# A conditioned four-layer sequence kernel: the first layer's query and key weights loaded as eight transfers instead of two

## The reference, cut to what matters

```python
mod = silu(c) @ W_mod + b_mod                    # six vectors of 128 per batch
sh_msa, sc_msa, g_msa, sh_mlp, sc_mlp, g_mlp = split(mod, 6)
h = layernorm(x) * (1 + sc_msa) + sh_msa
q, k, v = split(h @ W_qkv, 3)                    # 16 heads of 64
x = x + g_msa * (softmax(q k^T / 8) v @ W_out + b_out)
x = x + g_mlp * ff(layernorm(x) * (1 + sc_mlp) + sh_mlp)
```

## Time and profile before

| | |
|---|---|
| three runs, device time | 498.73, 500.25, 500.51 us; median 500.25 |
| the profiled execution, device time | 498.17 us |
| its span, first to last instruction | 496.4 us |
| mean granted TensorE clock in it | 0.965 of full speed |
| busy: PE, PEld, DVE, ACT, POOL | 410.4, 261.3, 310.9, 280.1, 175.7 us |
| moved by DMA | 21.25 MB |

### The profile page before, as it was taken

How to read it: one execution, slowest core, us unless ns; L and a number is a source line. 1 busy time by engine, 2 the same in 40 slices (tenths; PEclk the granted TensorE clock), 3 DMA queues, 4 the chain that set the end, 5 groups by cost and what they waited for, 6 DMA issues and landing times. The chain is left out here.

```text
span 496.4 us, 9353 instructions
## 1 busy us (share of the span) xinstructions
PE 410.4 (83%) x3196; PEld 261.3 (53%) x3196; DVE 310.9 (63%) x846; ACT 280.1 (56%) x596; POOL 175.7 (35%) x226
## 2 busy tenths in 40 slices
PE   4767788898889998889988788787688889799965
PEld 4534454555546555455545455445355666666644
DVE  4656776764573455726475766867688877675621
ACT  2333344375453846346755776456568566877754
POOL 7503211331263331774379222723133322321210
PEclk9999899999999999999997989879899999999997
DMA  6860033000000000120013030001222313210000
GB/s 160 303 61 2 9 30 48 1 1 1 0 1 2 1 1 12 45 73 2 0 33 85 13 101 27 3 1 41 87 75 87 96 34 98 82 59 12 3 12 11
DMA packets 34527, 21.25 MB, mean 43 GB/s; under 512 B 22832, under 2 KB 31408, under 8 KB 34096
## 3 DMA queue, kind: packets, MB, share of 16 engines
q1 hardware_dynamic: 34480, 20.65, 16.1%
HBM read 16.97 MB, written 3.67 MB: 42 GB/s over the span
## 5 line engine op out<-in xcount | busy, mean ns | idle before, releaser
L917 ACT ACTIVATE pt<-psum 128x512 f32<-128x512 f32 (+1 forms) x192 | 106.2, 558 | 95.5 <-PE psum L1514 47.2
L1121 DVE TENSOR_REDUCE negm<-psum 128x2 f32<-128x512 f32 x128 | 84.6, 683 | 38.5 <-PE psum L1443 24.7
L703 POOL TENSOR_TENSOR pairsum<-pt 128x256 f32<-128x256 f32 x64 | 46.8, 732 | 143.6 <-ACT pt L917 140.2
L714 POOL COPY big<-mT 32x1024 bf16<-32x1024 bf16 x32 | 33.2, 1038 | 119.4 <-ACT mT L909 119.0
L1489 PE MATMUL psum<-big 128*128 128x256 bf16 (+1 forms) x256 | 50.8, 268 | 4.8 <-POOL big L714 3.7
L1118 DVE TENSOR_REDUCE negm<-psum 128x3 f32<-128x384 f32 x64 | 34.8, 554 | 15.1 <-PE psum L1449 14.4
L1509 PE MATMUL psum<-big 64*128 64x256 f32 x256 | 40.1, 404 | 2.5 <-ACT pt L917 2.4
L1162 DVE TENSOR_TENSOR oT<-psum,rden 128x256 f32<-128x256 f32 x64 | 26.5, 415 | 18.8 <-ACT rden L933 18.2
L1538 PE MATMUL psum<-pt,room 128*64 128x256 f32 x256 | 35.6, 400 | 0.0
L1412 PE MATMUL psum<-hT,pt 128*128 128x256 f32 x128 | 33.3, 396 | 1.4 <-DVE negm L1121 1.3
L1538 PE MATMUL psum<-pt,vpad 128*32 128x256 f32 (+1 forms) x512 | 32.5, 373 | 1.6 <-DVE oT L1162 1.6
(11 more groups left out here) (184 smaller groups left out, 858.9 us busy)
## 6 DMA issues: line engine op xcount, KB each, us to landing
big<-scratch SPq DMA_DIRECT2D x96, 96.0 KB
scratch<-room SPq DMA_DIRECT2D x48, 64.0 KB, 2.0
adj_s<-adj SPq DMA_DIRECT2D x16, 110.0 KB, 3.7
w0s<-w SPq DMA_DIRECT2D x1, 1536.0 KB, 8.3
w3s<-w SPq DMA_DIRECT2D x1, 1088.0 KB, 10.9
room<-wqk SPq DMA_DIRECT2D x2, 512.0 KB, 6.3
xT<-x_t SPq DMA_DIRECT2D x4, 128.0 KB, 2.2
w1s<-w SPq DMA_DIRECT2D x1, 512.0 KB, 8.9
```

Source lines behind the costliest of these rows:

```text
L703: nc.gpsimd.tensor_tensor(pairsum[:, u % SUM_RING, :], pt[:, pt_slot(u), 0:T], pt[:, pt_slot(u), T:2 * T], ALU.add).then_inc(pairsum_ready, 1)
L714: nc.gpsimd.tensor_copy(stacks[SHIFT_ROW:128, b % ROOMS, 0, GH * g:GH * (g + 1), :], mT[SHIFT_ROW:128, at % 2, :].unsqueeze(1).broadcast_t ...
L917: nc.scalar.activation(pt[:, pt_slot(u), 0:width], psum[:, ST_BANK + u % 2, 0:width], ACT.Exp, scale=EXP_SCALE[layer]).then_inc(pt_ready, 1)
L1121: ins = nc.vector.tensor_reduce(negm[:, g, 0:NT, j], bk.rearrange("p (q k) -> p q k", q=NT), AX_X, ALU.max, negate=True)
```

## The change

The two transfers become eight. Each carries four heads of the queries or of the keys: 64 rows of 2 KB, 128 KB in all. They are issued in the order queries 0 to 3, keys 0 to 3, queries 4 to 7, and so on. The one semaphore becomes four, one for each group of four heads, and `turn_weights(n)` waits for its own group's two transfers alone. SP still waits for all eight before it goes on.

```diff
-        wqk_in = sem("wqk_in")
+        wqk_in = [sem(f"wqk_in{n}") for n in range(W_PARTS)]
...
-                for s in range(2):
-                    sp.dma_start(wqk0s[s * DH0:(s + 1) * DH0], wqk0[:, s]).then_inc(wqk_in, 16)
-
-                sp.wait_ge(wqk_in, 16 * 2)
+                for n in range(W_PARTS):
+                    heads = slice(H // W_PARTS * n, H // W_PARTS * (n + 1))
+                    for s in range(2):
+                        sp.dma_start(wqk0s[s * DH0:(s + 1) * DH0, heads], wqk0[:, s, heads]).then_inc(wqk_in[n], 16)
+
+                for n in range(W_PARTS):
+                    sp.wait_ge(wqk_in[n], 16 * 2)
...
                 def turn_weights(n):
 
-                    pe.wait_ge(wqk_in, 16 * 2)
+                    pe.wait_ge(wqk_in[n], 16 * 2)
                     wait_s_bank_free(pe, "W", n)
```

## The result

| | before | after |
|---|---|---|
| median of 22 runs each, us | 499.13 | 497.24 |
| ratio, 95% interval | | 0.9946 (0.9923 to 0.997) |
| profiled execution, us (span) | 498.17 (496.4) | 494.97 (493.2) |
| mean granted clock in it | 0.965 | 0.969 |

The ratio leaves out the slow runs of either kernel (four of the 22 of after) and says 0.54% less time, 2.7 us (1.5 to 3.8); over all 22 of each the medians differ by 1.9 us. Forecast were 1.3 us, 0.26%. The direction and the place were right, the forecast size was half of what the ratio says.

What follows compares the result with a forecast made beforehand. The head was taken to be bound by PE's 1.92 us wait for the query and key weights, then DVE. A shift of 1.3 us, taken between 1.1 and 1.4, gave 500.25 - 1.3 = 498.9 us, range 496.8 to 500.8.

Steps and rivals of the forecast that it cites:

- Where the gain comes from: PE behind first_mods: its 1.92 us standstill is its only wait on the query and key weights.
- Landings (part 1): Query and key transfers: eight issues take 3.8 us; pairs land no later than 6.9, 8.2, 9.5 and 10.8.
- Rival (a): Small transfers do not overlap, so turn_weights(3) waits; last lands at 19, kernel 6 us later at 506.3 us; chance 4%.
- The most that this edit can give is 1.92 us: Upper bound at the head of the chain: PE's whole idle time from 8.05 to 9.97.
- Part 2: PE's turning of the weights: transposes from 8.05, third group 10.2 to 11.3, ACT's second copy from 12.98 to 11.4.
- part 3: DVE is late next: vectors until 10.39, xn until 11.03, unmoved; last weight loads at 11.8, first product at 12.7; shift 1.3 us.
- DVE in the way whatever lands: Argument against a larger gain: DVE is occupied from 8.10 to 11.03 however early the weights land.
- rival (c): Faster by over 0.5%: the whole 1.92 us arrives and low-clock stretches fall better, about 497 us; chance 14%.
- The clock: Granted at 1.00 (2.4 GHz) in the first 30 us; low-clock stretches can differ by execution and cause spread.
- part 4: Everything behind the first product follows: no later wait is ended by SP's transfers or POOL, so the shift reaches the end.
- The sum: Whole kernel: no PE, DVE or ACT instruction added or removed; 500.25 - 1.3 = 498.9 us, a gain of 0.26%.
- What a measurement can tell: Measurement of this kernel: about 0.5% (2.5 us) can be told from no change; the runs' spread is 1.8 us.

Runs made afterwards that it cites:

- e1: Changed kernel with its eight transfers, but the first group of transposes waits for all four pairs; ratio to before 0.9988 (0.9949 to 1.0026).
- e5: Changed kernel once more, unedited, for a second profile; ratio to before 0.9984 (0.9942 to 1.0025).
- e6: Changed kernel with eleven more identity transposes in PE's earlier idle times; ratio to before 0.995 (0.9924 to 0.9975).
- e8: Changed kernel with eleven more identity transposes on PE and six small DVE instructions moved behind the copy of part 1; ratio to before 0.9952 (0.9917 to 0.9987).
- e11: Changed kernel with four transfers of 256 KB instead of eight, two weight parts waiting for each pair; ratio to before 0.9957 (0.992 to 0.9994).
- e12: Changed kernel with six small DVE instructions moved behind the copy of part 1 and POOL's mask building held back; ratio to before 0.9927 (0.9891 to 0.9964).
- e9: Kernel before, unedited, run again as a measure of scatter; ratio to its own runs 0.9944 (0.9908 to 0.9979).
- e4: Changed kernel with POOL's later mask building held back until the modulation vectors are done; ratio to before 0.9937 (0.99 to 0.9974).
- e10: Kernel before with POOL's later mask building held back until the modulation vectors are done; ratio to before 0.9962 (0.9926 to 0.9998).
- e2: Kernel before with eight identity transposes added to fill PE's idle 1.92 us behind first_mods; ratio to before 1.0021 (0.9986 to 1.0056).
- e3: Changed kernel with two more copies from PSUM on DVE ahead of xn; ratio to before 1.0028 (0.9992 to 1.0064).
- e15: Kernel before, unedited, sent again for the scatter between equal kernels; ratio to before 0.9995 (0.9963 to 1.0027).
- e14: Changed kernel, unedited, sent beside the unedited kernel before; ratio to before 0.9955 (0.9912 to 0.9998).
- e7: Changed kernel with six of DVE's eleven small modulation instructions moved behind the copy of part 1; ratio to before 0.9932 (0.989 to 0.9974).
- e16: Changed kernel, unedited, sent again for the scatter between equal kernels; ratio to before 0.9948 (0.9908 to 0.9989).

## Why the prediction was off

- **Where the gain comes from**: right. It is PE's idle time behind `first_mods`; e1 gives it back.
- **Landings (part 1)**: right within bounds (pairs at 6.7, 7.6, 9.3 and 10.0; upper bounds 6.9, 8.2, 9.5 and 10.8). The issue cost was too low (0.6 instead of 0.47 us each, 5.04 us for eight instead of 3.8), which SP's own wait covered. The last pair landed by 10.1. Rival (a), transfers paid one after the other, did not come: issued 0.63 us apart, each landed 3.1 to 3.9 us after its issue.
- **"The most that this edit can give is 1.92 us"**: wrong by 0.2. The transposes began at 7.85, not at 8.05, because their weight loads no longer wait and overlap the last modulation products (PEld from 7.64).
- **Part 2**: mis-added. In the earlier trace rows the loads of part 2 start 1.86 us behind the first transpose and ACT's second copy 3.01 us behind it. From 8.05 that gives 9.91 and 11.06, where I wrote 10.2 and 11.4. Measured were 9.68 and 10.83. The same rows have the product 4.12 us behind the first transpose: 8.05 + 4.12 = 12.2, not 12.7, as long as nothing but PE and ACT holds it. That sum was never made.
- **"DVE's modulation vectors: 8.10 to 10.39; none of it moves"** (part 3): this is the step that failed, DVE as what holds part 3 and with it the product. I took 2.29 us, one profile's duration of eleven small instructions, as a fixed cost. It is 1.40 us on its own and 1.75 to 2.30 by how it meets POOL. With 2.29 (e5) the forecast chain holds almost to the letter: the copy of part 1 at 10.92 (forecast 11.0), part 3's loads at 11.71 (11.8), `hT` at 11.69 (11.9). With 1.75 DVE is out of the way, part 3's loads start at 11.13 and the product at 11.94, not 12.7. Between e5 and after lie 0.37 us; at the lower clock it would be about 0.5 (an estimate: part 3's loads from 11.71, 0.72 us long as in after, put the product at 12.45). The other 0.25 us to 12.7 is mostly the length of part 3's loads: 0.72 us, where I had taken 0.87 from the kernel before. The "DVE in the way whatever lands" that spoke against rival (c) fell with it: of the rivals, (c), given 14%, has the mechanism that came. That the ratio passed its 0.5% is in part luck: 2.3 us at equal clock are 0.46%.
- **The clock**: I read 1.00 in the windows as 2.4 GHz for the first 30 us. The head ran at the 1.2 GHz level, and in e5 the rise at 11.37 took part 3 from 1.06 to 0.63 us, worth some 0.15 us to the product (12.31 against the 12.45 above). Over the four profiles of each unedited kernel the rise came at 14.1 to 16.3 before and 11.2 to 12.5 after; but e6, e8, e11 and e12, with the same head start, rose at 13.7 to 14.1. That the change moves the rise is likely and not shown.
- **The rest (part 4)**: right. The shift of 2.1 us, 2.45 with the faster first products, stayed until the clock's stretches differed (from 260 us on). Nothing behind SP's wait was late.
- **The sum**: 2.1 us from four profiles of each (first product at 14.20 on average against 12.10), where I had 1.3. The error is in parts 2 and 3 and in the 0.2 us at the start of the transposes; the signs of all steps held.
- **What a measurement can tell**: I had taken the scatter of three runs, 1.8 us. A set of twelve differed from the 35 runs of the same kernel beside it by up to 0.56% (e9).

## What to carry to other kernels

When a wait is taken away, the time to the next one is a sum of durations that were slack before, and nobody had a reason to look at how steady they are: take for each the shortest that a row of the same operation shows as well as the one in its place. Cutting a load pays as far as its consumer can start on a part, here with one cut in two, though with 0.05 us to spare. And where a kernel's runs scatter by as much as the change moves it, compare runs with the same granted clock, and send the unedited kernel along as a control.

## What the runs showed of the hardware

- **DVE beside POOL.** A DVE instruction of 0.16 us on 128x4 elements took up to 0.54 us while POOL ran memsets and selects on on-chip memory, and 0.16 again when POOL was held back (e4, e10). The Trainium skill, page "SBUF — State Buffer", section "SBUF: two separate sides", states that the engines' side of that memory has contention only at the port that VectorE and GpSimd share. e4 agrees with it as far as the delay goes with POOL's work; which port it is, no run here shows. Whether the small instructions started 0.13 or 0.05 us ahead of POOL's memset went with 0.54 us more or less for the eleven together.
- **The profile's clock before its first rise.** It reads 1.00, while float32 transposes of 128x128 take 421 to 434 ns, as they do where the record grants 0.50, against 273 later. In a stretch at the start of a kernel the durations of a known matmul are the better witness.
- **Low stretches of the clock early in the kernel.** The windows from 16 to 48 us of the kernel before, first profile, and of e9, the same kernel:

```profile
16.00:48.00 32.00, 23.39 (x145) 13.43 (x143) 19.66 (x57) 12.04 (x26) 6.78 (x9) 1.00 0.47 108
```

```profile
16.00:48.00 32.00, 23.95 (x125) 13.16 (x124) 17.68 (x42) 11.80 (x25) 6.76 (x9) 0.89 0.48 105
```

  With 0.89 the late modulation products came at 46.0 instead of 43.4. Such a stretch, starting between 17.5 and 32.4 us, stood in e1, e2, e3, e6, e8, e9, e10, e11 and e15, and is why the markers of e1, e6 and e11 (45.3, 46.1, 46.3) say nothing about their edits; in none of the four profiles of the changed kernel did one stand before 48.7 us (e14 was granted 0.95 at best over the whole execution, a third level of its own). They go with a late first rise of the clock: none of the six profiles whose rise came before 13.0 us (after, e4, e5, e7, e14, e16) has one, nine of the twelve that rose at 13.4 or later do. Which of the two brings the other, or a third thing both, was not found.
